# State rows of a selective scan from DRAM broadcasts, with output sums moved into the recurrences

## The reference

```python
xz = x @ in_proj_w.T
xs, z = jnp.split(xz, 2, axis=-1)            # xs then through a short convolution and silu
dbc = xs @ x_proj_w.T
dt = softplus(dbc[..., :DT_RANK] @ dt_proj_w.T + dt_proj_b)
Bm, Cm = dbc[..., DT_RANK:DT_RANK + D_STATE], dbc[..., DT_RANK + D_STATE:]
dA  = jnp.exp(dt[..., None] * A)
dBu = dt[..., None] * Bm[:, :, None, :] * xs[..., None]
hs  = scan(h[t] = dA[t] * h[t-1] + dBu[t])
y = (jnp.einsum('blds,bls->bld', hs, Cm) + xs * Dvec) * silu(z)
return y @ out_proj_w.T
```

## Time and profile before

| what | value |
|---|---|
| runs | 664.46 us median of 3 (664.15 to 665.54) |
| span of the profiled execution | 663.5 us, first to last instruction |
| DVE, PE, POOL, ACT busy in it | 527.6, 496.2, 349.8, 320.8 us |
| mean granted clock of TensorE | 0.839 of full speed |
| moved by DMA | 8.35 MB, mean 13 GB/s |
| first scan starts, last scan ends | 307.05 us, 526.18 us |

### The profile page before, as it was taken

The page is one execution under the profiler, slowest core; times in us unless marked ns, Lnnn a source line. Parts: engine busy times, 40 slices in busy tenths (PEclk is TensorE's granted clock), DMA queues, the critical chain, the costliest instruction groups (busy, mean ns, idle before and its releaser), DMA issues.

```text
span 663.5 us, 7944 instructions
## 1 busy us (share of the span) xinstructions
PE 496.2 (75%) x2663; PEld 303.8 (46%) x2663; DVE 527.6 (80%) x831; ACT 320.8 (48%) x380; POOL 349.8 (53%) x198
## 2 busy tenths in 40 slices
PE   2896989898994999786877888788788997723200
PEld 2255869787884874232333333233233583422200
DVE  4999996996699350677989999789999648687897
ACT  2441323415340227877878677667777505621220
POOL 5262342553233000256778888689978806777303
PEclk9796669986895899998989999899999977855555
DMA  6410000000000001000000000000000001012100
GB/s 198 101 36 1 0 1 2 2 11 0 1 9 1 9 9 36 0 0 1 0 0 0 1 0 0 0 0 0 1 0 0 1 1 17 10 8 8 5 0 32
DMA packets 17969, 8.35 MB, mean 13 GB/s; under 512 B 14832, under 2 KB 17168, under 8 KB 17680
## 3 DMA queue, kind: packets, MB, share of 16 engines
q1 hardware_dynamic: 16144, 7.35, 4.1%
q0 software_dynamic: 1792, 0.58, 1.5%
HBM read 6.67 MB, written 1.25 MB: 12 GB/s over the span
## 4 chain that ended last, share of the span: by engine, by line
DVE 33%; PE 29%; POOL 14%; issue 13%; ACT 9%; DMA 2%; DVEq 0%; POOLq 0%; ACTq 0%; SPq 0%
POOL arena L569 8%; PE ps L640 7%; PE ps L813 5%; POOL arena L531 5%; DVE arena L1566 5%; DVE ps L1556 4%; DVE arena L1345 3%; PE ps L662 3%; DVE arena L1360 2%; PE ps L688 2%; PE ps L806 1%; DVE arena L1391 1%; PE ps L778 1%; PE ps L625 1%; PE ps L746 1%
## 5 line engine op out<-in xcount | busy, mean ns | idle before, releaser
L531 POOL TENSOR_TENSOR arena<-arena 128x1024 f32<-128x1024 f32 x64 | 149.9, 2355 | 35.5 <-PE ps L813 14.4
L1566 DVE TENSOR_TENSOR_SCAN arena<-arena,ps 128x1024 f32<-128x1024 f32 x64 | 144.6, 2280 | 6.7 <-ACT arena L1082 0.6
L813 PE MATMUL ps<-arena,ident 128*128 128x512 f32 x256 | 126.1, 621 | 11.8 <-POOL arena L531 11.6
L496 POOL TENSOR_TENSOR arena<-arena 128x1536 f32<-128x1536 f32 (+2 forms) x16 | 65.9, 4122 | 108.3 <-DVE arena L1249 57.8
L640 PE MATMUL ps<-arena 128*128 128x64 f32 x576 | 81.1, 311 | 12.4 <-DVE x_tok L1277 12.4
L1091 ACT ACTIVATE arena<-ps 128x1024 f32<-128x1024 f32 x64 | 65.4, 1021 | 44.3 <-PE ps L806 25.0
L640 PEld LDWEIGHTS ps<-arena 128*128 128x128 f32 x576 | 80.2, 227 | 12.8 <-issue 12.8
L813 PEld LDWEIGHTS ps<-arena,ident 128*128 128x128 f32 x256 | 48.4, 197 | 65.1 <-issue 37.8
L569 POOL DMA_INDIRECT arena<-node_rows,src_idx x56 | 56.4, 1006 | 37.2 <-DMA node_rows<-hrow 20.5
L1082 ACT ACTIVATE arena<-arena,neg_a 128x1020 f32<-128x1020 f32 x64 | 72.9, 1139 | 3.8 <-DVE arena L1548 2.1
L1556 DVE TENSOR_TENSOR ps<-arena,ps 128x1024 f32<-128x1024 f32 x48 | 58.1, 1211 | 12.4 <-PE ps L798 12.3
(11 more groups left out here) (345 smaller groups left out, 798.0 us busy)
## 6 DMA issues: line engine op xcount, KB each, us to landing
arena<-dram_edges SPq DMA_DIRECT2D x2, 1024.0 KB, 8.7
arena<-dram_x SPq DMA_DIRECT2D x2, 512.0 KB, 4.8
arena<-node_rows,src_idx POOLq DMA_INDIRECT x56, 2.8
x_tok<-dram_x SPq DMA_DIRECT2D x1, 512.0 KB, 11.0
res_scratch<-x_tok SPq DMA_DIRECT2D x4, 128.0 KB, 2.0
arena<-res_scratch SPq DMA_DIRECT2D x1, 512.0 KB, 3.3
w<-dram_w SPq DMA_DIRECT2D x3, 128.0 KB, 2.6
arena<-dram_f_conv_w SPq DMA_DIRECT2D x1, 256.0 KB, 11.1
```

The source lines that it names most:

```text
L496: g.tensor_tensor(s_buf[i % 2][:, kk], wy[:, i, kk].unsqueeze(3).to_broadcast([P, nk, HEIGHT, WIDTH]), wx[:, i, kk].unsqueeze(2).to_broadc ...
L531: g.tensor_tensor(gg[r % 2], hh[r % 2], cs[r % 2], ALU.mult).then_inc(s["g_ready"], 1)
L813: m = pe.matmul(ps[:, 4 + q, :], ident[:], gg[e][:, 512 * q:512 * q + 512], start=False, stop=True, skip_group_check=True)
L1566: v.tensor_tensor_scan(o, x0, x1, 0.0, ALU.mult, ALU.add).then_inc(s["scan_ready"], 1)
```

## The change

`rows_c`, `b_copy` and ACT's copies of C rows are gone. Instead DVE copies the 32 B and C rows of each direction in fp32 from PSUM to SBUF (`state_rows`, on partitions 64 to 95 over `r1`), SP writes them to DRAM (`row_d`, 256 KB for each direction), and SP brings each C row (`c_row`, into one of four buffers `cs`) and each fourth B row (`b_row`, into `bx`) back with a transfer that reads one row of 4 KB for all 128 partitions: 64 + 16 transfers of 512 KB written. `cs[2]` lies where `t2` lies later, `cs[3]` is new. POOL takes `own_b(0)` ahead of the second direction's L512 and L514. The last product with C is made by DVE, not POOL. TensorE's order becomes `rows(n)`, then `add_state(n - 3)`; with banks 2 and 3 free, the residual and forward projection of token groups 0 to 11 run in block 2 (from its fifth state), and the backward projection is cut in two halves of 64 columns, the first of which runs for groups 0 to 11 in block 3. The first B row is made ahead of TensorE's filler matmuls. All loops over states are written out.

```diff
+            def row_of(n, i0):
+                d, c0 = n // (2 * DS), (n // DS) % 2 * HALF
+                return row_d[d, i0:i0 + 1, c0:c0 + HALF].to_broadcast([P, HALF])
+            def b_row(grp):
+                if grp:
+                    sp.wait_ge(s["bx_put"], grp)
+                n = GROUP * grp + GROUP - 1
+                sp.dma_start(bx, row_of(n, n % DS)).then_inc(s["bx_in"], 16)
+            def c_row(n):
+                if n >= GROUP:
+                    sp.wait_ge(s["g_ready"], n - GROUP + 3)
+                sp.dma_start(cs[n % GROUP], row_of(n, DS + n % DS)).then_inc(s[f"c_in{n % GROUP}"], 16)
+            for d in range(2):
+                sp.wait_ge(s["rows_kept"], 2 * d + 2)
+                sp.dma_start(row_d[d], state_rows).then_inc(s["rows_out"], 16)
+                sp.wait_ge(s["rows_out"], 16 * d + 16)
+                if d == 0:
+                    b_row(0)
+                    for n in (0, 1, 3):
+                        c_row(n)
+            sp.wait_ge(s["dt_ready"], 2)
+            c_row(2)
+            for n in range(GROUP, STATES):
+                c_row(n)
+                if n % GROUP == 0:
+                    b_row(n // GROUP)
...
+            def own_b(grp):
+                d, c0 = grp // (2 * GROUP), grp // GROUP % 2 * HALF
+                g.wait_ge(s["bx_in"], 16 * grp + 16)
+                g.tensor_tensor(bx, uu[d][:, c0:c0 + HALF], bx, ALU.mult).then_inc(s["bx_ready"], 1)
+            def with_c(n):
+                g.wait_ge(s["scan_ready"], n + 3)
+                g.wait_ge(s[f"c_in{n % GROUP}"], 16 * (n // GROUP) + 16)
+                g.wait_ge(s["g_used"], n + 1)
+                g.tensor_tensor(gg[n % 2], hh[n % 2], cs[n % GROUP], ALU.mult).then_inc(s["g_ready"], 1)
...
                 g.wait_ge(s["dt_ready"], d + 1)
                 g.tensor_tensor(uu[d], dtv[d], xs[d], ALU.mult).then_inc(s["uu_ready"], 1)
+                if d == 0:
+                    g.wait_ge(s["uu_ready"], 1)
+                    own_b(0)
...
+            def out_backward(j, half):
+                at = slice(C * half, C * half + C)
+                return pe.matmul(token_out(j, at), zs[1][:, HALF * half + j:HALF * half + HALF:NPO], o_w[1][:], start=False, stop=True,
+                                 tile_position=(0, C * half), skip_group_check=True)
...
+            for n in range(STATES):
+                blk, i = n // DS, n % DS
...
+                if n and n % GROUP < GROUP - 1:
+                    rows(n)
+                if n == 1:
+                    skip_path(0)
+                elif i == 3 and blk:
                     pe.wait_ge(s["yg_ready"], blk)
                     skip_path(blk)
+                if n >= 3:
+                    add_state(n - 3)
+                if blk == 2 and i >= 4:
+                    j = i - 4
+                    if j % 2 == 0:
+                        out_rest(j)
+                    out_forward(j)
+                elif blk == 3 and i >= 4:
+                    out_backward(i - 4, 0)
+            add_state(STATES - 3)
+            pe.wait_ge(s["scan_ready"], STATES + 1)
+            for j in range(early, NPO):
+                if j % 2 == 0:
+                    out_rest(j)
+                out_forward(j)
+            add_state(STATES - 2)
+            add_state(STATES - 1)
+            for j in range(early, NPO):
+                out_backward(j, 0)
             pe.wait_ge(s["yg_ready"], 4)
...
                     v.wait_ge(s["hi_ready"], 2 * d + hf + 1)
+                    if d and hf == 0:
+                        v.wait_ge(s["rows_out"], 16)
+                    v.tensor_copy(state_rows[:, cols], ps[C:C + 2 * DS, 4 - 4 * d + 2 * hf:6 - 4 * d + 2 * hf, :].rearrange("p b n -> p (b n)")).then_inc(s["rows_kept"], 1)
                     tt(r1[:, cols], banks(4 - 4 * d + 2 * hf, 2, 64), bc3[d][0:64, cols], ALU.subtract).then_inc(s["rest_ready"], 1)
...
+            v.wait_ge(s["scan_ready"], STATES + 2)
+            v.wait_ge(s["c_in3"], 16 * (STATES // GROUP))
+            v.wait_ge(s["g_used"], STATES)
+            tt(gg[1], hh[1], cs[GROUP - 1], ALU.mult).then_inc(s["last_ready"], 1)
             gated(3)
```

More of the change, by code:

```diff
@@ L820, in skip_path, with token_out, out_rest, out_forward @@
                     pe.matmul(ps[:, 4 + q, :], diag_d[d][:], xs[d][:, c0 + 512 * q:c0 + 512 * q + 512], start=True, stop=True)
-            def first_rows(blk):
-                d, hf = blk // 2, blk % 2
-                pe.wait_ge(s["bc_ready"], d + 1)
-                rows_c(d, hf, slice(GROUP - 1, GROUP), 4 * blk * SLOTS)
-                for e in range(2):
-                    rows(d, hf, slice(e, e + 1), 16 * blk + e, e)
-                    if e == 0 and blk == 0:
-                        skip_path(0)
-                    rows_c(d, hf, slice(DS + e, DS + e + 1), 4 * blk * SLOTS + 1 + e)
+            def token_out(j, parts=slice(0, P)):
+                j0, j1, bank = J_BANK[J_GROUP[j]]
+                return ps[parts, bank, FOLD * (j - j0):FOLD * (j - j0) + FOLD]
+            def out_rest(j):
+                j0, j1, bank = J_BANK[J_GROUP[j]]
+                pe.matmul(ps[:, bank, FOLD * (j - j0):FOLD * (j - j0) + 2 * FOLD], res_t[:, j // 2, :], fold, start=(j == j0), stop=True,
+                          skip_group_check=True)
+            def out_forward(j):
+                pe.matmul(token_out(j), zs[0][:, j:T:NPO], o_w[0][:], start=False, stop=True, skip_group_check=True)
+            def out_backward(j, half):
+                at = slice(C * half, C * half + C)
+                return pe.matmul(token_out(j, at), zs[1][:, HALF * half + j:HALF * half + HALF:NPO], o_w[1][:], start=False, stop=True,
+                                 tile_position=(0, C * half), skip_group_check=True)
+            early = J_BANK[2][0]
+            pe.wait_ge(s["bc_ready"], 1)
+            pe.wait_ge(s["z_ready"], 1)
+            rows(0)
             pe.wait_ge(s["z_ready"], 3)
@@ L836, in _ @@
             pe.wait_ge(s["diag_ready"], 2)
-            first_rows(0)
-            for blk in range(4):
-                d, hf = blk // 2, blk % 2
-                rows(d, hf, slice(2, 3), 16 * blk + 2, 0)
-                rows_c(d, hf, slice(DS + 2, DS + 3), 4 * blk * SLOTS + 3)
-                rows_c(d, hf, slice(DS + 3, DS + 4), 4 * blk * SLOTS + 4)
-                if blk:
+            pe.wait_ge(s["rest_t_ready"], 1)
+            for n in range(STATES):
+                blk, i = n // DS, n % DS
+                if n == 2 * DS:
+                    pe.wait_ge(s["bc_ready"], 2)
+                if n and n % GROUP < GROUP - 1:
[3 more added lines that the diff above has]
+                elif i == 3 and blk:
@@ L845, in _ @@
                     pe.wait_ge(s["yg_ready"], blk)
                     skip_path(blk)
-                for e in range(2):
-                    add_state(16 * blk + e, e)
-                with pe.Fori(0, DS // GROUP - 1) as it:
-                    n, slot = it * GROUP + 16 * blk, it * SLOTS + (4 * blk + 1) * SLOTS
-                    rows_c(d, hf, bass.ds(it * GROUP + 7, 1), slot)
-                    for r in range(GROUP):
-                        if r < GROUP - 1:
-                            rows(d, hf, bass.ds(it * GROUP + (4 + r), 1), n + (4 + r), r % 2)
-                        rows_c(d, hf, bass.ds(it * GROUP + (DS + 4 + r), 1), slot + (1 + r))
-                        add_state(n + (2 + r), r % 2)
@@ L1093, in _ @@
-            act.wait_ge(s["nega_ready"], 4)
-            for d in range(2):
-                act.wait_ge(s["dt_ready"], d + 1)
-                act.wait_ge(s["da_zero"], 2 + d)
-                lo = 1 - d
-                for hf in range(2):
-                    blk, c0 = 2 * d + hf, hf * HALF
-                    src = dtv[d][:, c0:c0 + HALF].rearrange("p (b s) -> p b s", s=SEQ)[:, :, lo:lo + SEQ - 1]
-                    with act.Fori(0, DS // GROUP) as it:
-                        states(it + 4 * blk, src, lo, d, lambda r: bass.ds(it * GROUP + r, 1))
+            act.wait_ge(s["nega_ready"], 4)
@@ new lines, in _ @@
+            for n in range(STATES):
+                d, c0, lo = n // (2 * DS), n // DS % 2 * HALF, 1 - n // (2 * DS)
+                if n % (2 * DS) == 0:
+                    act.wait_ge(s["dt_ready"], d + 1)
+                    act.wait_ge(s["da_zero"], 2 + d)
+                act.wait_ge(s["scan_ready"], n + 1)
+                f(da[n % 2].rearrange("p (b s) -> p b s", s=SEQ)[:, :, lo:lo + SEQ - 1],
+                  dtv[d][:, c0:c0 + HALF].rearrange("p (b s) -> p b s", s=SEQ)[:, :, lo:lo + SEQ - 1], ACT.Exp,
+                  scale=neg_a[d][:, n % DS:n % DS + 1]).then_inc(s["da_ready"], 1)
+                if n % GROUP == GROUP - 1:
+                    act.wait_ge(s["bx_ready"], n // GROUP + 1)
+                    f(banks(6, 2), bx, ACT.Copy).then_inc(s["bx_put"], 1)
```

126 lines of the change are left out of this document (34 added, 92 removed).

## The result

The changed kernel takes 646.98 us, the median of 4 runs (645.19 to 648.33), beside 665.0 us for the kernel before in the same session; the ratio is 0.9727, 95% interval 0.9707 to 0.9747. The forecast was 650.0, with a range of 643 to 660. The profiled execution took 647.57 us and has a span of 645.8, 17.7 us less than the 663.5 of the earlier trace rows.

The account below looks back on a forecast made before the run. DVE was taken to bound the recurrences, with 11.4 us of stalls. Gains of 0.2 at the start, 8.4 in the recurrences and 6.0 at the end made 14.6, so 664.46 - 14.6 = 649.9, rounded 650.0; range 643 to 660.

Parts of the forecast that it names:

- The bound of the recurrences: Recurrences: DVE binds, needing 12.83 us in each of 16 groups, 207.7 us in all, so 11.4 of 219.1 are stalls.
- Four falls of the clock at 0.7 us: Recurrences: TensorE's clock drops to its half level four times, each costing DVE 0.7 us of stall, 3 us together.
- rival 1: Blocks 0 and 1: TensorE's clock falls in nearly every group, eating the recurrences' gain; 658 us, chance 0.18.
- the walk: Instruction-by-instruction schedule: TensorE waits 1.75 us per group, first scan at 306.85, third statistics part 12.15 us after the last scan.
- Transfers at nothing: Recurrences: the broadcast transfers of B and C rows add no time, covered by 6 and 10 us before use.
- The reserve: DMA engines in the recurrences: 204 GB/s asked, half of the 410 reached; a 512 KB transfer lands in 3.3 us.
- Rival 2: DMA engines with SP's queue: transfers bind above 2.57 us each; without overlap 3.3 us each, 709 us; chance 0.11.
- The start: Up to the first scan: four added DVE copies of 1.15 us, dt 2.4 us later, first scan 306.85, gain 0.2.
- The end: Last scan to third statistics part: early projection sums shorten 18.5 us to 12.15; gain 6.4, taken as 6.0.
- Rival 3: Recurrences: b_row's chain is 0.9 us late in each group, 14.4 us eat the gain, no visible change, 664; chance 0.05.

## Why the forecast was right, step by step

- **The bound of the recurrences, 207.7 us from one group of 12.83: right, a little high.** With all but 0.6 us of the stalls gone they took 207.9, so the bound is 207.3; in the changed kernel 210.4 - 3.4 = 207.0.
- **Four falls of the clock at 0.7 us: right in kind and in sum, not in the parts.** The trace shows half-clock stretches at 311 to 321, 328 to 331, 341 to 345, 355 to 359 and 420 to 423 us and stalls of 3.4 us, where 3 was taken. The stalls that follow them are about 1.5, 0.6, 0.2, 0 and 1.1 us, so 0.7 is a mean and no price of one fall. Four lie in the first block (to 358 us), so they don't recur in each group of the place that rival 1 named. Ahead of these four TensorE stood idle for 2.05 to 2.60 us, longer than the 1.75 of the walk; waits for GpSimd or VectorE within later groups were 1.6 us or less, and no fall followed them. The fifth came at a place that the step didn't name: a skip sum waited 2.33 us for the gating there. Waits of 2.33 us at the two other gatings were followed by none. That the gain of 8.7 us is so near the 8.4 is partly luck: the bound was 0.7 us too high and the stalls 0.4 too low.
- **Transfers at nothing: right.** Leaving them out changes nothing. The reserve was smaller than the step said: the share was 0.57 where it had half, and the landing 4.3 us where it took 3.3. Whether a steady stream of broadcasts keeps up 410 GB/s isn't shown; with as many copies to DRAM beside them 240 was kept up. Rival 2's point is 2.57 us for each transfer; the changed kernel's share gives an estimate of 0.57 x 211 / 75 = 1.6, the mix took 2.2.
- **The start: right, with its mechanism.** The dt chain came 2.5 us later (VectorE's memset from 301.36 to 303.87), and the first scan at 306.70 where the walk had 306.85. The four copies took 1.22 us each, in place of 1.15. What the walk has as a wait stands within VectorE's rows: GpSimd's own B product ended at 290.50, and the cast, 1.22 us long elsewhere, at 290.07 + 1.51 = 291.58, 0.14 short of 290.50 + 1.22; GpSimd's subtraction ended at 295.73, and L1538, 1.20 long alone, at 296.82, 0.11 short of 295.73 + 1.20. That L1538's length comes from GpSimd's instruction is shown by moving that.
- **The end: right in kind, its walk 1.95 us too long (12.15 for 10.2), and with 6.0 taken for the 6.4 of the walk it makes 2.3 of the 3 us missed.** The rest is 0.3 in the recurrences, 0.15 at the start and 0.3 in the stretch that was to stay as it was. In the end two terms were off. The half instruction was put at 0.14 us, "nearer to half", and took 0.118: 32 x 0.022 = 0.7. The last four token groups of residual and forward sums were walked from -0.1 to 2.4 us around the last scan's end; they ran from -1.2 to 1.0 (TensorE's L861 and L866 at 515.84 to 518.0), since the state sum ahead of them had ended at -1.1, and what follows came 1.4 sooner: the gating ended at 5.9 in place of 7.3. Of these 2.1 us 1.95 reach the third part.
- **Rival 3** (the B row's chain a little late) didn't come, but the run with the later issue shows its place and, for a row that is 3.2 us late in each group, a price of 46.7 us; the rival's 14.4 were for 0.9 us. A late row that GpSimd releases itself stays late in every group.

## What to carry to other kernels

Before a transfer is put beside compute, ask who releases its issue, and how far ahead of the use: if it is the engine that will wait for the data, and it does so one instruction ahead, each landing stands on its path once a round, and no slack is ever built up. Size a queue's reserve from a long stretch full of the same kind of transfer, not from the highest short window. In one version an edit that gained 1.6 us at the start lost 3.5 behind the statistics, in a stretch that it doesn't touch, so compare untouched stretches too.

## What was not expected of the hardware

- In the version with the copies behind the cast TensorE stood at the half clock from 545 to 560 us although it was busy for 15.00 of the 15.00 us, while the changed kernel had 1.00 in the same window at 12.43 busy. In the run with fillers there the clock was 0.99 to 545 us, TensorE then waited 2.7 us for ScalarE, and it stood at 0.50 through 14.98 of 15 busy us. What decides the level in this stretch these runs don't show.
- A matmul of 84 moving fp32 columns took 0.118 us with 64 stationary columns and 0.227 with 128, back to back with its weight loads. With 128 the pace was the same, six or seven a microsecond, at a granted clock of 1.00 and of 0.50.
- Broadcasting transfers, one DRAM row of 4 KB to 128 partitions, went on at 240 GB/s for 280 us at a share of 0.90 together with as many that wrote the same rows to DRAM, and landed 17.4 us after issue there, against 4.3 at 188 GB/s alone.
